# A down projection of fp32 halves as seven products of half matrices, on one Trainium2 core

## The reference, cut to what matters

```python
weights = _routing_weights(x, Wr, temperature)      # [1, 1250, 8]
gate = jnp.einsum('btd,edi->beti', x, Wg)           # 8 experts, I = 128
up = jnp.einsum('btd,edi->beti', x, Wu)
h = jax.nn.silu(gate) * up
e_out = jnp.einsum('beti,eid->betd', h, Wd)
out = jnp.einsum('bte,betd->btd', weights, e_out)
x = x + out
```

## Time and profile before

| | |
|---|---|
| median of 3 runs | 1101.96 us (1101.73 to 1101.97) |
| the profiled execution | 1102.07 us |
| its span, first to last instruction | 1100.1 us |
| PE busy | 1089.3 us, 99% |
| DVE busy | 374.4 us, 34% |
| ACT busy | 251.4 us, 23% |
| POOL busy | 294.0 us, 27% |
| mean granted TensorE clock | 1.000 |

### The profile page before, as it was taken

How to read it: one execution, slowest core, us unless ns; L and a number is a source line. 1 busy time by engine, 2 the same in 40 slices (tenths; PEclk the granted TensorE clock), 3 DMA queues, 4 the chain that set the end, 5 groups by cost and what they waited for, 6 DMA issues and landing times.

```text
span 1100.1 us, 15031 instructions
## 1 busy us (share of the span) xinstructions
PE 1089.3 (99%) x5647; PEld 903.7 (82%) x5647; DVE 374.4 (34%) x996; ACT 251.4 (23%) x398; POOL 294.0 (27%) x243
## 2 busy tenths in 40 slices
PE   8999999999999999999999999999999999999998
PEld 7887778887888888888788888887788888888887
DVE  6944656675631111322211223444321111111111
ACT  5320211121232344211111113334131111112000
POOL 4000011121141356300054445343142222235000
PEclk9999999999999999999999999999999999999999
DMA  7203012222243586504199987764032222215321
GB/s 266 96 29 106 13 35 59 67 70 67 66 146 119 188 287 218 187 1 153 42 277 322 292 234 204 232 190 140 1 87 62 62 62 62 74 59 212 115 96 67
DMA packets 145977, 139.28 MB, mean 127 GB/s; under 512 B 7958, under 2 KB 115826, under 8 KB 145650
## 3 DMA queue, kind: packets, MB, share of 16 engines
q1 hardware_dynamic: 145330, 136.48, 39.7%
q10 hardware_dynamic: 576, 1.84, 0.5%
HBM read 102.32 MB, written 35.96 MB: 126 GB/s over the span
## 4 chain that ended last, share of the span: by engine, by line
PE 95%; DVE 3%; DMA 1%; ACT 1%; issue 1%; SPq 0%; ACTq 0%; DVEq 0%
PE ps L1590 9%; PE ps L1592 9%; PE ps L1591 9%; PE ps L1890 7%; PE ps L1891 7%; PE ps L1892 7%; PE ps L1831 4%; PE ps L1825 4%; PE ps L1805 3%; PE ps L1756 3%; PE ps L1807 3%; PE ps L1806 3%; PE ps L1938 3%; PE ps L1939 3%; PE ps L1758 3%; PE ps L1940 3%
## 5 line engine op out<-in xcount | busy, mean ns | idle before, releaser
L1590 PE MATMUL ps<-w_hi,xnH 128*128 128x512 f32 x464 | 184.6, 398 | 0.0
L1592 PE MATMUL ps<-w_hi,xnL 128*128 128x512 f32 x464 | 180.9, 390 | 0.0
L1591 PE MATMUL ps<-w_lo,xnH 128*128 128x512 f32 x464 | 180.7, 389 | 0.0
L736 POOL TENSOR_TENSOR acc<-acc,cw 128x320 f32<-128x320 f32 x40 | 35.8, 894 | 252.6 <-ACT cw L920 251.5
L1590 PEld LDWEIGHTS ps<-w_hi,xnH 128*128 128x128 f32 x464 | 87.1, 188 | 18.7
L1592 PEld LDWEIGHTS ps<-w_hi,xnL 128*128 128x128 f32 x464 | 87.1, 188 | 18.5
L1591 PEld LDWEIGHTS ps<-w_lo,xnH 128*128 128x128 f32 x464 | 87.2, 188 | 17.2
L1543 DVE TENSOR_TENSOR prd<-ps,wB 128x512 f32<-128x512 f32 (+1 forms) x24 | 14.2, 592 | 161.9 <-PE ps L1892 147.8
L1756 PE MATMUL ps<-xnH,w_hi 128*128 128x512 f32 (+1 forms) x192 | 68.1, 355 | 0.0
L1890 PE MATMUL ps<-x2H,guH 128*128 128x512 f32 (+1 forms) x192 | 67.7, 352 | 0.4 <-ACT wT L1100 0.4
L1891 PE MATMUL ps<-x2L,guH 128*128 128x512 f32 (+1 forms) x192 | 67.6, 352 | 0.0
(11 more groups left out here) (316 smaller groups left out, 2068.7 us busy)
## 6 DMA issues: line engine op xcount, KB each, us to landing
cR<-c_d SPq DMA_DIRECT2D x20, 640.0 KB, 5.0
foldin<-in SPq DMA_DIRECT2D x32, 256.0 KB, 2.7
guR<-in SPq DMA_DIRECT2D x16, 512.0 KB, 5.4
w_raw<-in SPq DMA_DIRECT2D x14, 512.0 KB, 6.7
c_d<-cw SPq DMA_DIRECT2D x40, 160.0 KB
qs0H<-qT_d SPq DMA_DIRECT2D x10, 512.0 KB, 5.3
qs0L<-qT_d SPq DMA_DIRECT2D x10, 512.0 KB, 6.6
ob<-x_d SPq DMA_DIRECT2D x20, 256.0 KB, 2.7
```

The source lines that it names most:

```text
L1590: pe.matmul(target, xnH[:, kc, cols], wH[w][:, kc, :], start=(kc == 0), stop=False)
L1591: pe.matmul(target, xnH[:, kc, cols], wL[w][:, kc, :], start=False, stop=False)
L1592: mm = pe.matmul(target, xnL[:, kc, cols], wH[w][:, kc, :], start=False, stop=(kc == KC - 1))
```

## The change

The two operands are cut in four. Of the tokens h, half k (0 or 1) is four experts, and a token tile r or r + 5 is the upper or lower half of the ten token tiles (HALF = 5). The weights are cut by experts and by columns. Seven products of such halves, some of them of sums and differences, take the place of eight. Each product q has 5 steps r (one token tile of the upper or lower half), each step 4 x 3 matmuls into one bank. Products 1 and 2 (q = 0, 1) add up in one bank, as do q = 3 and 4, and q = 5 and 6.

- The tokens stay fp32: `product` writes them to hT directly, and `hidden_high` and `hidden_low` are gone. Each of 35 steps splits its operand when it is used, in one of three small buffers: `token_high` on ScalarE, `token_low` on VectorE. The buffer of step i is free when step i - 3 is done.
- Sums of tokens (`first_sums`, `third_sum`, `fourth_sum`: 20 operations of 128x512) are made by VectorE between the steps.
- Weights are seven panels of 128x2048 (q = 0 to 6). Panels 0, 1, 3 and 6 are loaded (3 becomes a difference), 2, 4 and 5 are sums; VectorE makes panel 2 in two operations (`second_panel`), GpSimd makes 3, 4 and 5 in one each. ScalarE's `down_high` and GpSimd's `down_low` split each. Panels 0 and 1 are split in the expert stage.
- ScalarE copies the first product out (`first_product_out`), VectorE adds products 3 and 4's banks to it (u2, u3), GpSimd adds u2 or u3 to the x in ob (`add_earlier`, 15 times), and VectorE adds the bank to that (`result`, 20 times).

The diff, cut:

```diff
-            def load_d0(k):
-                sp.wait_ge(up_mm, 3 * (NEXP - 1 + k))
...
+                if n == 3:
+                    load_down(wdR[0], 0, 0, 0)
+                if n == 9:
+                    load_down(wdR[1], 1, 0, 1)
+                if n == 22:
+                    sp.wait_ge(up_mm, 3 * (NEXP - 1))
+                    load_down(wdR[3], 0, 1, 2)
+                    load_down(wdR[6], 1, 1, 3)
...
+            sp.wait_ge(up_mm, 3 * NEXP)
+            load_down(wd_low_left, 1, 0, 4)
...
 POOL
-            def hidden_low(n):
...
+            def down_low(q):
+                pool.wait_ge(wd_hi, q + 1)
+                pool.tensor_tensor(wdL[q][:], wdR[q][:], wdH[q][:].bitcast(F32), ALU.subtract).then_inc(wd_lo, 1)
...
+            for e in range(2, NEXP):
+                gu_low(e)
+                if e in (4, 6):
+                    down_low((e - 4) // 2)
+
+
+            pool.wait_ge(in_d[2], 16)
+            pool.wait_ge(in_d[3], 16)
+            pool.tensor_tensor(wdR[3][:], wdR[6][:], wdR[3][:], ALU.subtract).then_inc(wd_mix, 1)
+            pool.wait_ge(wd_t2, 2)
             down_low(2)
+            pool.wait_ge(in_d[4], 16)
+            pool.tensor_tensor(wdR[4][:], wd_low_left[:], wdR[2][:], ALU.subtract).then_inc(wd_mix, 1)
+            pool.tensor_tensor(wdR[5][:], wdR[6][:], wdR[2][:], ALU.subtract).then_inc(wd_mix, 1)
+            for q in range(3, 6):
+                down_low(q)
+
+            def add_earlier(d):
+
+                u, r = (u2, u3, u2)[d // HALF - 1], d % HALF
+                pool.wait_ge(in_o[d % 4], 16 * (d // 4 + 1))
+                pool.wait_ge(u_ok, (0, HALF, 0)[d // HALF - 1] + r + 1)
+                pool.tensor_tensor(ob[:, d % 4, :], ob[:, d % 4, :], u[:, r, :], ALU.add).then_inc(o_sum, 1)
+
+            for d in range(HALF, HALF + 3):
+                add_earlier(d)
+            down_low(6)
+            for d in range(HALF + 3, 2 * NT):
+                add_earlier(d)
...
 ACT
-            def hidden_high(n):
...
+            def token_high(i):
...
+                if i == 2:
+                    act.wait_ge(up_mm, 3 * NEXP)
+                if i >= 3:
+                    act.wait_ge(d_mm, i - 2)
+                act.activation(hxH[i % 3][:], hx_source(i), ACT.Copy).then_inc(hx_hi, 1)
...
+                if n in (7, 13):
+                    down_high((n - 7) // 6)
+                if n in (20, 21):
+                    token_high(n - 20)
+
+
+            for i in range(2, 7 * HALF):
+                token_high(i)
+                if 3 <= i < 3 + HALF:
+                    first_product_out(i - 3)
+                if i in (5, 7, 10, 13, 16):
+                    down_high({5: 2, 7: 3, 10: 4, 13: 5, 16: 6}[i])
...
 DVE
+                dve.tensor_tensor(hT[n // 12][:, n // 3 % 4, first:last], prd[:, n % 2, 0:cols], sil[:, n % 2, 0:cols],
+                                  ALU.mult).then_inc(prod_step, 1)
+
+            def token_low(i):
+                dve.wait_ge(hx_hi, i + 1)
+                dve.tensor_tensor(hxL[i % 3][:], hx_source(i), hxH[i % 3][:].bitcast(F32), ALU.subtract)\
+                   .then_inc(hx_lo, 1)
...
+            def first_sums(r):
+                dve.tensor_tensor(hs1[:, r], tokens(0, r + HALF), tokens(1, r + HALF), ALU.add).then_inc(hs, 1)
+                dve.wait_ge(hs, 2 * r + 1)
+                dve.tensor_tensor(hs2[:, r], hs1[:, r], tokens(0, r), ALU.subtract).then_inc(hs, 1)
...
+            dve.wait_ge(prod_step, 48)
+            dve.wait_ge(pads, 5)
+            for i in range(2, 7 * HALF + 3):
+                if i < 7 * HALF:
+                    token_low(i)
+                if i >= 3:
+                    product_out(i - 3)
+                if i in (2, 3):
+                    second_panel(i - 2)
+                if 4 <= i < 4 + HALF:
+                    first_sums(i - 4)
+                if 9 <= i < 9 + HALF:
+                    third_sum(i - 9)
+                if 18 <= i < 18 + HALF:
+                    fourth_sum(i - 18)
...
 PE
+            def down(q, r):
+                i, target = q * HALF + r, down_bank(GROUP[q], r)
+                bank_is_free(q, r)
+                if r == 0:
+                    pe.wait_ge(wd_lo, q + 1)
+                pe.wait_ge(hx_lo, i + 1)
+                opens = q not in (1, 4, 6)
+                for k in range(4):
+                    hi, lo = hxH[i % 3][:, k, :], hxL[i % 3][:, k, :]
+                    high, low = wdH[q][:, k, :], wdL[q][:, k, :]
+                    pe.matmul(target, hi, high, start=(opens and k == 0), stop=False, skip_group_check=not opens)
+                    pe.matmul(target, hi, low, start=False, stop=False, skip_group_check=not opens)
+                    mm = pe.matmul(target, lo, high, start=False, stop=(k == 3), skip_group_check=not opens)
+                mm.then_inc(d_mm, 1)
+
+            for q in range(7):
+                for r in range(HALF):
+                    down(q, r)
```

More of the change, by code:

```diff
@@ L43 @@
 FIRST_WIN_STEP = NT + 1
+HALF = NT // 2
 CHUNKS = ((0, 512), (512, 1024), (1024, 1250))
@@ L235, in x2L, with tokens, hx_source, down_out @@
             return x2L0[:, kc, :] if kc < 4 else xnL[:, kc, :]
[L237 to L240, removed]
+        def tokens(k, t):
+            return hT[k][:, :, t * P:(t + 1) * P]
+        def hx_source(i):
+            q, r = divmod(i, HALF)
+            return (lambda: tokens(0, r), lambda: tokens(1, r), lambda: hs2[:, r], lambda: tokens(0, r + HALF),
+                    lambda: tokens(1, r + HALF), lambda: hs1[:, r], lambda: tokens(1, r))[q]()
+        def down_out(d):
+            return (0, d) if d < NT else (1, (d - HALF) % NT)
         ps = nc.alloc_psum_tensor("ps", [P, 8 * BANK], F32)
@@ L254, in gps_layer, with down_bank @@
         D_BANK = (0, 1, 5, 6, 2, 3, 4, 7)
+        def down_bank(group, r):
+            return bank(D_BANK[(group * HALF + r) % 8])
         in_x = [sem(f"in_x{k}") for k in range(3)]
@@ L283, in gps_layer @@
         in_gu = [[sem(f"in_gu{k}_{g}") for g in range(2)] for k in range(2)]
-        in_d = [sem(f"in_d{k}") for k in range(6)]
+        in_d = [sem(f"in_d{k}") for k in range(5)]
         in_o = [sem(f"in_o{k}") for k in range(4)]
@@ L357, in gps_layer @@
         prod_step = sem("prod_step")
[L358 to L361, removed]
+        wd_mix = sem("wd_mix")
+        wd_t2 = sem("wd_t2")
+        wd_hi = sem("wd_hi")
+        wd_lo = sem("wd_lo")
+        hs = sem("hs")
+        hx_hi = sem("hx_hi")
+        hx_lo = sem("hx_lo")
+        p1_out = sem("p1_out")
+        u_ok = sem("u_ok")
+        o_sum = sem("o_sum")
         d_mm = sem("d_mm")
@@ L674, in _ @@
                 load_o(d)
[L675 to L677 removed]
             for d in range(2 * NT):
[L679 removed]
+                hf, t = down_out(d)
                 sp.wait_ge(d_dr, d + 1)
@@ L829, in _ @@
             for e in range(2):
                 gu_low(e)
[L831 to L842, removed]
@@ L844, in _ @@
-            down_low(1)
-            down_low(2)
+            pool.wait_ge(a_done, 2 * NT)
+            for k in range(2):
+                pool.memset(hT[k][:, :, N:NP], 0.0).then_inc(pads, 1)
+            for e in range(2, NEXP):
[5 more added lines that the diff above has]
+            pool.tensor_tensor(wdR[3][:], wdR[6][:], wdR[3][:], ALU.subtract).then_inc(wd_mix, 1)
@@ L1086, in gate, with down_high, first_product_out @@
                 act.activation(sil[:, n % 2, 0:cols], bank(PAIR[n % 4][0], cols), ACT.Silu).then_inc(silu_done, 1)
-            def hidden_high(n):
[L1089 to L1092, removed]
+            def down_high(q):
+                if q < 2:
+                    act.wait_ge(in_d[q], 16)
+                elif q == 2:
+                    act.wait_ge(wd_t2, 2)
+                elif q < 6:
+                    act.wait_ge(wd_mix, q - 2)
+                act.activation(wdH[q][:], wdR[q][:], ACT.Copy).then_inc(wd_hi, 1)
+            def token_high(i):
+                q, r = divmod(i, HALF)
+                if q == 0:
+                    act.wait_ge(prod_step, 24)
+                elif q in (1, 4):
+                    act.wait_ge(prod_step, 48)
+                    act.wait_ge(pads, 5)
+                else:
+                    act.wait_ge(hs, {2: 2 * r + 2, 3: 2 * HALF + r + 1, 5: 2 * r + 1, 6: 3 * HALF + r + 1}[q])
+                if i == 2:
[3 more added lines that the diff above has]
+                act.activation(hxH[i % 3][:], hx_source(i), ACT.Copy).then_inc(hx_hi, 1)
+            def first_product_out(r):
+                act.wait_ge(d_mm, r + 1)
+                act.activation(u2[:, r, :], down_bank(0, r), ACT.Copy).then_inc(p1_out, 1)
             act.wait_ge(rt, 1)
@@ L1550, in _ @@
             for n in range(24):
                 product(n)
[L1554 to L1557, removed]
+                if n in (21, 22):
+                    token_low(n - 21)
+            def first_sums(r):
```

(55 more changed lines are left out.)

67 lines of the change are left out of this document (23 added, 44 removed).

## The result

The changed kernel takes 1112.12 us (median, 1111.6 to 1113.49), the kernel before 1101.9: ratio 1.0095, 95% interval 1.0077 to 1.0112. The forecast was 1105.5 us, slower: the sign came out, the size did not. The profiled execution took 1113.49 us, the longest of the four.

A forecast was written before the change was run, and what follows sets the result against it. TensorE, busy 99% of the span, was taken to bound the kernel. Saving, turns, later stalls, starts anew and clock: -13.6 + 12.6 + 1.9 + 0.5 + 2.0 = +3.4 us on 1102.07, giving 1105.5 us; 8-in-10 range 1097 to 1111.

The forecast's parts named there:

- TensorE's saving: Down projection: 420 matmuls instead of 480 save 13.6 us, so the whole stage would take 95.2 us.
- The turns on the port: Down stage, before step 7: VectorE gets one two-SBUF-operand operation after each of four GpSimd subtractions, stalling TensorE 12.6 us.
- Rows 8 to 11: Earlier kernel's profile rows, read as VectorE operations on two SBUF operands and GpSimd ones excluding each other, taking turns.
- Later stalls: Down stage, near steps 10 to 14: single GpSimd operations hold up token lows, costing 1.9 us.
- The clock: Behind the long TensorE stall in the down stage: matmuls run at a lowered clock, costing 2.0 us.
- starts anew: Down stage: TensorE starts anew three times at 0.2 us each, 0.5 us in all.
- The end: After result 15: last add waits some 7 us and has 10.9 us, so the tail after the last matmul stays unchanged.
- Rival 3: Down stage, slower still: later stalls 5.4 us instead of 1.9, clock 5.4 instead of 2.0, 1112 us; chance 0.08.

The follow-up runs named there:

- experiment 2: Changed kernel with GpSimd filling five low panels and two difference panels with zeros instead of computing them, leaving out those parts of the product: 1096.03 us, one execution.
- experiment 3: Changed kernel with GpSimd's 128x2048 subtractions in the down stage made in four pieces of 128x512: 1105.41 us, ratio 1.0032.
- experiment 5: Kernel of experiment 1 with GpSimd's subtractions whole but spread out, each waiting for a given TensorE step: 1097.72 us, ratio 0.9965.
- experiment 6: Kernel of experiment 1 with VectorE making the first and third token sums four steps later: 1108.08 us, ratio 1.0053.
- Experiment 8: Kernel of experiment 1 with 50 unread matmuls into an unused bank before step 7: 1106.32 us, ratio 1.0040.
- experiment 1: Changed kernel with SP's queue loading the x of output d + 3 after the store of output d is issued: 1105.71 us, ratio 1.0036.
- experiment 7: Kernel of experiment 1 with GpSimd's subtractions cut by urgency into 2, 4 or 8 pieces: 1089.87 us, ratio 0.9891.
- experiment 4: Changed kernel with the queue order of experiment 1 and GpSimd's subtractions in eight pieces of 128x256: 1091.67 us, ratio 0.9909.

## Why the prediction was right or wrong

- **TensorE's saving, right.** With the stall gone (experiment 2) the stage is 95.2 us, as worked out.
- **The turns on the port, right in place, size and cause.** Forecast: token low 7 ends 31.6 us into the stage, a stall of 12.6. Trace: step 7 starts 31.7 us in, TensorE waits 11.8 for that token low and 0.3 for the one before. Rows 8 to 11 held for operations of 4.6 us too. Experiments 2, 3 and 5 show it is GpSimd's reading, its piece size and its row of four; experiment 6 shows it is not VectorE's order.
- **Later stalls, right.** 1.9 us forecast; 1.8 waited for, at step 14.
- **The clock, too low.** 2.0 us forecast. The gaps, 14.5 us in all (with the starts anew, 0.5 us as forecast), and 95.2 us of work leave 3.8 of the 113.5 us. Of these, 3.6 us are in step 7 (4.6 us instead of 2.72) and in steps 14 and 15 (4.2 and 3.0): the short stall near step 14 dropped the clock too. Experiment 8 shows that taking part of this away need not show in the end.
- **The end, wrong: this is the step that failed.** The prediction put it: "At the end the last add waits on a store (2.0), a load (2.7) and GpSimd (1.3) after result 15, some 7 us, and has four steps (10.9 us). The tail after the last matmul stays what it is." So the tail was put at +0, and it measured +6.8 us. The sum in that sentence is the round trip of one buffer, as if the queue stood ready. But SP's queue is one line: it waits for each store to land before it loads, and it loads before it sees the next store. Result 15 starts at 1093.24 and ends at 1093.94, yet its store is issued only at 1100.12, 6.2 us later. The pace of the queue is not the round trip divided by four, but store wait plus load, 3.6 us an output. Before, outputs came every 24 matmuls, 5.4 us, and the queue stood idle in between:

```profile
1070.37 0.34 SPq L681 DMA_DIRECT2D out<-ob  x1
1072.42 0.32 SPq L668 DMA_DIRECT2D ob<-x_d  x1
1075.81 0.34 SPq L681 DMA_DIRECT2D out<-ob  x1
```

The seven products bunch the last 15 outputs at one per 12 matmuls, 2.72 us. From the first load that this holds up to the last there are ten outputs, each some 0.9 us in arrears; less some 2 us by which the first was early, that is about the 6.8 us (an estimate from the timelines). Moving each load behind the next store gives 6.4 us back (experiment 1).

Without that term the mechanism of the forecast stands. That its time of 1105.5 us also lies within 0.2 us of the 1105.71 of the kernel whose queue keeps up is partly luck: the stage is still 1.2 us longer than the sum had it (1.8 us more for the clock, 0.5 less for the gaps), and that kernel's executions spread from 1105.35 to 1106.74. Rival 3 named 1112 us, which is what the changed kernel took, but not for its reasons: it had 5.4 us of later stalls and 5.4 us of clock, against 1.8 and 3.8 measured, and no change at the end. With the operations cut and the queue reordered the change is worth 12 us (experiment 7); the port and the queue cost it 22.

## What to carry to other kernels

When work moves from TensorE to VectorE and GpSimd, count the operations that need their shared port as one engine's, and look at what stands in a row: pieces no longer than the buffers' cover, the most urgent in the smallest. For each queue, ask at what pace the new schedule asks it for work, with every wait in its order, and not only how long one item takes. A schedule with the same bytes but outputs bunched at the end can turn a hidden queue into the bound.

## What the runs showed of the hardware that was not expected

- A GpSimd fill of 128x2048 (1.81 us) does not hold VectorE's operations on two SBUF operands (0.68 to 0.69 us beside it), a subtraction does. By the Trainium skill (SBUF — State Buffer, "Who interferes with whom") only GpSimd instructions that read SBUF contend with them; the trace agrees.
- A store of 256 KB landed in 2.0 us before; in the kernel after, mostly issued right behind a load of the same queue, it landed in 3.2 us (median of the last 15).
- Handing the port over costs GpSimd mostly 0.43 to 0.45 us, for pieces of 128x256 as for 128x2048 (1.19 us instead of 0.75 in experiment 4, 5.04 instead of 4.6 in the kernel after, where two others took 4.94).
- The clock did not follow the length of a gap alone: behind a wait of 1.8 us near step 14 it fell (kernel after, 0.66 from 1042.2 to 1046.4), behind waits of 2.1 us in experiment 4 and 2.0 us in experiment 8 it stayed at 1.00.
